# Dot attention on one core: score tiles of 128x64 in pairs in place of 128x128

## The reference

```python
q = x1.reshape(n, 8, -1).transpose(1, 0, 2) * 64 ** -0.5      # x1: result of the first layer
k = x2.reshape(n, 8, -1).transpose(1, 0, 2)
vv = v.reshape(n, 8, -1).transpose(1, 0, 2)
scores = jnp.einsum('hnd,hmd->hnm', q, k)
scores = jnp.where(adj > 0, scores, NEG_FILL)
attn = jax.nn.softmax(scores, axis=-1)
out = jnp.einsum('hnm,hmd->hnd', attn, vv)                      # then residual and layernorm
```

## Time and profile before

| | us |
|---|---|
| median of 3 runs (4103.87 to 4105.66) | 4104.07 |
| the profiled execution, its own time | 4103.82 |
| span of its trace, first to last instruction | 4102.3 |
| `attend_dot` on PE, first to last score matmul | 2012.2 to 3929.6 |

### The profile page before, as it was taken

How to read it: one execution, slowest core, us unless ns; L and a number is a source line. 1 busy time by engine, 2 the same in 40 slices (tenths; PEclk the granted TensorE clock), 3 DMA queues, 4 the chain that set the end, 5 groups by cost and what they waited for, 6 DMA issues and landing times. The chain is left out here.

```text
span 4102.3 us, 55678 instructions
## 1 busy us (share of the span) xinstructions
PE 3871.6 (94%) x19385; PEld 1354.5 (33%) x19385; DVE 3128.7 (76%) x3078; ACT 2527.7 (62%) x2396; POOL 1525.1 (37%) x1115
## 2 busy tenths in 40 slices
PE   7887999999999999976699999999999999999987
PEld 5564222222222222235333333333333333333345
DVE  5555999999999999978677677676777676677656
ACT  3444888888888888842255555555555555555520
POOL 3332000000000000015467666666766666676620
PEclk9998999999999999975799999999999999999975
DMA  7875111111111111136699999999999999999864
GB/s 272 295 275 181 39 40 40 49 45 40 41 39 39 52 44 39 41 118 233 160 183 185 191 190 192 190 190 184 185 190 192 190 190 188 186 184 192 179 170 144
DMA packets 339912, 592.36 MB, mean 144 GB/s; under 512 B 29248, under 2 KB 201280, under 8 KB 339776
## 3 DMA queue, kind: packets, MB, share of 16 engines
q0 software_dynamic: 84224, 302.29, 37.5%
q1 hardware_dynamic: 238400, 262.89, 21.2%
q10 hardware_dynamic: 17152, 25.43, 1.8%
HBM read 262.70 MB, written 59.38 MB: 79 GB/s over the span
## 5 line engine op out<-in xcount | busy, mean ns | idle before, releaser
L1117 DVE TENSOR_TENSOR a_weights<-a_psS,maskT 128x1024 f32<-128x1024 f32 x1024 | 1205.6, 1219 | 582.1 <-ACT a_psS L1082 582.1
L1082 ACT ACTIVATE a_psS<-a_psS,a_shift 128x1024 f32<-128x1024 f32 x1024 | 1071.7, 1084 | 801.3 <-PE a_psS L1010 801.2
L477 ACT ACTIVATE g_weights<-al_bc,g_shift,g_xl 128x1024 f32<-128x1024 f32 x1024 | 1187.8, 1232 | 166.7 <-DVE g_total L523 80.4
L516 DVE TENSOR_TENSOR g_weights<-g_weights,maskT 128x1024 f32<-128x1024 f32 x1024 | 1175.6, 1218 | 97.5 <-ACT g_weights L477 96.6
L1010 PE MATMUL a_psS<-a_q,a_k 128*128 128x512 f16 x4096 | 974.5, 381 | 18.0 <-DMA a_k<-k_scratch 16.6
L1027 PE MATMUL a_psO<-a_weights,a_v 128*64 128x512 f32 x4096 | 988.0, 604 | 0.0
L568 PE MATMUL g_psO<-g_weights,g_xl 128*64 128x512 f32 x4096 | 965.9, 603 | 17.8 <-DVE g_weights L516 17.8
L1140 POOL TENSOR_TENSOR a_pool_total<-a_pool_total,a_weights 128x1024 f32<-128x1024 f32 x336 | 898.5, 2674 | 0.0
L1010 PEld LDWEIGHTS a_psS<-a_q,a_k 128*128 128x128 f16 x4096 | 358.7, 98 | 798.5 <-DVE a_weights L1117 312.5
L1148 POOL DMA_DIRECT2D a_dma_total<-a_weights x480 | 415.9, 867 | 523.7 <-DVE a_weights L1117 415.3
L599 POOL DMA_DIRECT2D o_scratch<-g_o x16 | 8.9, 559 | 1387.9 <-ACT g_d L486 1387.9
(11 more groups left out here) (135 smaller groups left out, 1846.9 us busy)
## 6 DMA issues: line engine op xcount, KB each, us to landing
a_dma_total<-a_weights POOLq DMA_DIRECT2D x512, 512.0 KB, 5.1
adj_sb<-in_adj_dram SPq DMA_DIRECT2D x128, 512.0 KB, 5.5
g_xl<-xl_scratch SPq DMA_DIRECT2D x128, 260.0 KB, 2.8
a_k<-k_scratch SPq DMA_DIRECT2D x256, 128.0 KB, 5.1
a_v<-in_L_gnn_v_dram SPq DMA_DIRECT2D x128, 256.0 KB, 3.1
al_bc<-alpha_scratch SPq DMA_DIRECT2D x16, 1024.0 KB, 4.9
f_oT<-o_scratch SPq DMA_DIRECT2D x16, 1024.0 KB
a_q<-q_scratch SPq DMA_DIRECT2D x64, 256.0 KB, 6.9
```

Source lines behind the costliest of these rows:

```text
L477: nc.scalar.activation(w[:, u % NP, h, :], al_bc[:, par, h, :], ACT.Exp, bias=shift_bc[:, par, h:h + 1], scale=xl[:, slot, u % KB, 2 * C + ...
L516: nc.vector.tensor_tensor(w[:, u % NP, h, :], w[:, u % NP, h, :], maskT[:, ds(q * JB + u, 1), ds(ic * IC, IC)] .rearrange("p a c -> p (a c)"),
L1082: nc.scalar.activation(psS[n % RING][:], psS[n % RING][:], ACT.Exp, bias=shift_bc[:, g % 2, h:h + 1], scale=SCALE).then_inc(exped, 1)
L1117: nc.vector.tensor_tensor(w[:, u % NP, h, :], psS[n % RING][:].rearrange("p a c -> p (a c)"), maskT[:, j, (g // PAIRS) * IC:(g // PAIRS + ...
```

## The change

Each 128x128 score matmul becomes two with 64 stationary columns: keys 0 to 63 of the tile go to PSUM partitions 0 to 63, keys 64 to 127 to partitions 64 to 127. Moving operand, contraction, accumulation, banks, waits and the semaphore increment after the last matmul of a head stay. Per step there are 16 score matmuls in place of 8. Nothing else is changed.

```diff
                     for hf in range(2):
                         for part in range(2):
-                            last = nc.tensor.matmul(psS[n % RING][:, hf, :],
-                                                    k_sb[:, slot, h, (u % KB) * P:(u % KB + 1) * P],
-                                                    q_sb[:, par, part, h, hf * HALF:(hf + 1) * HALF],
-                                                    start=(part == 0), stop=(part == 1))
+                            for low in (0, C):
+                                keys = (u % KB) * P + low
+                                last = nc.tensor.matmul(psS[n % RING][low:low + C, hf, :],
+                                                        k_sb[:, slot, h, keys:keys + C],
+                                                        q_sb[:, par, part, h, hf * HALF:(hf + 1) * HALF],
+                                                        start=(part == 0), stop=(part == 1))
                     last.then_inc(scored, 1)
```

## The result

The changed kernel takes 3978.07 us (median of 4 runs, 3977.43 to 3980.04) against 4104.86 of the kernel before (median of 4 runs): ratio 0.9692, 95% interval 0.9675 to 0.9708, so 126.8 us less. The forecast was 3977, with 126.6 us as its sum. The profiled execution took 3977.43 us, 1.5 above its span of 3975.9.

A forecast was written before the change was run, and what follows sets the result against it. PE was taken to bound the dot stage, losing 0.256 us per step at tile changes. From 4103.8 us, 126.6 us removed and nothing added for pairs, loads or DMA gave 3977, range 3966 to 4044.

The forecast's parts named there:

- The pacemaker: Dot stage: PE alone sets the pace, busy throughout each 120.1 us group, at 3.70 us a step.
- The 0.256 us of a step: Dot stage: per 3.70 us step PE streams 3.44 us; the other 0.256 is lost where score and value blocks meet.
- fp16 in pairs costs nothing: Score block: a pair of 64-column fp16 matmuls takes the 0.216 us of one; one after the other would add 885 us.
- 494 pairs of borders x 0.256, plus one: Dot stage: tile changes removed between score and value blocks, 126.5 us, and 0.14 for the last entry: 126.6 us.
- Type fp32 to fp16: Border from values to scores: the type change was taken as free, though only the other direction was shown cleanly.
- DMA costed at 0: Dot stage: DMA share rises from 0.93 to 0.996 in a 112.2 us group, adding no time.
- my idea of the limit (1.07): DMA share isn't full at 1: windows of 7 and 11 us show 1.07 and 1.08, leaving engines at 93%.
- The slack of 7.2 us: Group's end: room for the last accumulating transfer before the denominators need it, 7.9 us before the change, about 7.2 after.
- DMA as a second bound: Rival 1, dot stage: with only a 0.98 share usable, groups take 114.0 us, total 4006; chance 0.09.
- half a gap left: Rival 2, score/value borders: type change or exposed first load keeps half the cost, 63 us, total 4041; chance 0.08.
- no change: Rival 3, score/value borders: fp16 and fp32 blocks differ in mode anyway, or any two blocks pay; 4104; chance 0.07.
- a dense pair that isn't dense: Rival 4, score block: loads take turns unhidden, pairs 0.274 us apart, 4214, or 4862 with no overlap; chance 0.08.

## Why the prediction was right

- **The pacemaker** (PE, by the distances between matmuls and not by its busy share): right. With the DMA demand a third lower the time stays at 3977.2. That PE never waited for the DMA engines was off by one wait of 2.3 us, at the stage's last denominators; it is 2.5 now.
- **The 0.256 us of a step sit at the two borders and go with the change of tile**: right, and shown by taking the change away with wide tiles (3977.0), by keeping it with half of the matmuls narrow (4089.8), by keeping half of the changes (4041.3), and by bringing it back with narrower tiles (4106.3).
- **fp16 in pairs costs nothing** (the term that the rows before did not show, bounded by 0.216 and 0.432): the low bound holds, 16 matmuls in 1.73 us, and the loads are hidden. The load itself came out at 110 ns.
- **494 pairs of borders x 0.256, plus one**: 126.6 against a measured 126.8; per group 112.2 as forecast. The mechanism and the size are right, but an agreement to 0.2 us is luck: the rows were read to 0.01 us, 10 us in the sum by the prediction's own reckoning, and the interval of the ratio is 7 us wide on each side.
- **Type fp32 to fp16**, which I had not seen as cleanly as the other way: no cost, by the wide values.
- **DMA costed at 0**: right for this kernel. Its share came out at 0.98, not 0.996, and my idea of the limit (1.07) was high; 1.05 is the most that a whole group showed. The room is thus at most 7% by 1.05 / 0.98, and one more copy or an even faster group already brings waits at the denominators. The slack of 7.2 us that I gave them was worked out with the median landing of 5.1; the slowest of these transfers took 9.2 us before and 10.1 after, so it is good only while the engines have room.
- **Rivals**: DMA as a second bound, half a gap left, no change, and a dense pair that isn't dense, all fell, each by a row or a run above.

## What to carry to other kernels

Where a PE-bound stage alternates between matmuls that use different parts of the array, compare the distance between block starts with the number of matmuls times their own distance; the rest, here 0.13 us for one change of tile on average (0.10 from 128*64 back to 128*128, 0.15 the other way, 0.14 either way in the graph attention), can be taken back by giving neighbours the same tile, split or widened, as long as the streaming stays the same. Prefer to change the tile rather than the order: here merging blocks to save changes held buffers longer and cost more than it saved. After the gain look at the next engine, which took over at once in one stage (DVE at 98%) and was at most 7% away in the other (DMA), close enough to eat up the last 0.26 us a group.

## What was unexpected of the hardware

- Two column halves of the array are not tied to each other by program order. Four matmuls of 0.216 us of one half ahead of the other's first delayed it by 0.03 us, not 0.65. How far one half can run ahead was not tried beyond these four, nor what a semaphore on the last matmul of one half says of the other half when they drift further apart.
- Waits of PE are paid twice when they are long enough for the clock to fall: after a 2.25 us wait in the graph attention a value block took 3.57 instead of 1.89 us, after 6.05 us in the dot attention a score block 2.83 instead of 1.89.
- 32 loads and 32 matmuls in 1.73 us, 0.027 us for each instruction, step after step, are no limit for PE's issue.
- The DMA share over whole groups did not pass 1.05, even with three more copies, though windows of 7 and 11 us show 1.07 and 1.08.
